# A scaled copy of the rows moved from VectorE to ScalarE, a rest of the context keys moved from GpSimd to VectorE, and first shared weights loaded one stage earlier

## The reference

```python
x = x + tanh(g_xattn[0]) * masked_attention(layernorm(x), ctx, mask, wq, wk, wv, wo, wg)   # 16 heads
x = x + tanh(g_ffn[0])   * ternary_linear(layernorm(x), weight, bias)
# second attention, for each sequence: Q = layernorm(x) [128 x 512], K = V = ctx [128 x 512]
s   = sigmoid(einsum('bdn,bdm->bnm', Q, K) / sqrt(128))        # 512 x 512
x   = x + tanh(g_xattn[1]) * einsum('bvn,bnm->bvm', V, s)
# 16 routed experts (4 for each row) and a shared expert of twice 352 hidden columns
xf  = layernorm(x)
z   = silu(xf @ sw1) * (xf @ sw3) @ sw2
x   = x + tanh(g_ffn[1]) * (routed_experts(xf) + z)
```

## Time and profile before

| | |
|---|---|
| Median of 3 runs | 1314.29 us |
| The profiled execution's own time | 1312.92 us |
| Its span | 1311.2 us |
| PE busy | 1218.4 us, 93% of the span |
| DVE, ACT, POOL busy | 684.4, 556.6, 433.5 us (52%, 42%, 33%) |
| Granted PE clock, mean | 0.979 of full speed |

### The profile page before, as it was taken

How to read it: one execution, slowest core, us unless ns; L and a number is a source line. 1 busy time by engine, 2 the same in 40 slices (tenths; PEclk the granted TensorE clock), 3 DMA queues, 4 the chain that set the end, 5 groups by cost and what they waited for, 6 DMA issues and landing times. The chain is left out here.

```text
span 1311.2 us, 25675 instructions
## 1 busy us (share of the span) xinstructions
PE 1218.4 (93%) x7835; PEld 1024.6 (78%) x7836; DVE 684.4 (52%) x1433; ACT 556.6 (42%) x1355; POOL 433.5 (33%) x518
## 2 busy tenths in 40 slices
PE   6998999999998888958999999899999999999995
PEld 6877787777786566745777787789999889999995
DVE  6556545545545698953656654633234553424241
ACT  4554455455455566723111111543334553434342
POOL 1102211211214466440002762244444344444433
PEclk9999999999999889979999999999999999999998
DMA  9100000000000011043000231665445666645454
GB/s 330 36 17 20 17 1 20 18 1 18 17 17 17 9 30 35 9 140 131 0 1 0 66 131 48 227 163 107 80 80 133 172 148 165 140 86 132 83 141 72
DMA packets 54335, 100.36 MB, mean 77 GB/s; under 512 B 5094, under 2 KB 21990, under 8 KB 54262
## 3 DMA queue, kind: packets, MB, share of 16 engines
q0 software_dynamic: 15824, 37.76, 15.2%
q1 hardware_dynamic: 38438, 61.65, 14.5%
HBM read 72.91 MB, written 26.48 MB: 76 GB/s over the span
## 5 line engine op out<-in xcount | busy, mean ns | idle before, releaser
L1828 PE MATMUL t_H<-m_W,t_xT 128*128 128x352 f32 x1632 | 280.3, 327 | 6.4 <-DVE m_W L1906 4.7
L1828 PEld LDWEIGHTS t_H<-m_W,t_xT 128*128 128x128 f32 x1632 | 261.7, 188 | 9.7 <-DVE m_W L1906 7.3
L1796 POOL DMA_INDIRECT out_dram<-t_ys,t_sid x68 | 109.5, 1610 | 220.9 <-ACT t_ys L1857 113.4
L688 ACT ACTIVATE pr<-SC,neg 128x128 f32<-128x128 f32 x256 | 89.9, 377 | 38.3 <-DVE neg L897 38.3
L1873 ACT ACTIVATE t_sl<-t_H 128x352 f32<-128x352 f32 x68 | 31.5, 463 | 174.0 <-PE t_H L1828 174.0
L46 PE MATMUL t_Y<-m_W,t_hT 128*128 128x512 f32 (+1 forms) x207 | 87.4, 422 | 5.4 <-issue 3.1
L1951 DVE TENSOR_TENSOR t_hT<-t_TH,t_hT 128x384 fp32r<-128x384 f32 x68 | 37.8, 556 | 102.0 <-ACT t_hT L1894 100.8
L1927 DVE TENSOR_TENSOR t_h<-t_H,t_sl 128x352 f32<-128x352 f32 x68 | 35.6, 523 | 103.3 <-ACT t_sl L1873 103.3
L1857 ACT ACTIVATE t_ys<-t_Y,t_wcol 128x512 f32<-128x512 f32 x69 | 47.3, 686 | 93.7 <-PE t_Y L48 93.7
L48 PE MATMUL t_Y<-m_W,t_hT 128*128 128x512 f32 (+1 forms) x207 | 81.7, 395 | 0.0
L47 PE MATMUL t_Y<-m_W,t_hT 128*128 128x512 f32 (+1 forms) x207 | 81.5, 394 | 0.0
(11 more groups left out here) (473 smaller groups left out, 3228.0 us busy)
## 6 DMA issues: line engine op xcount, KB each, us to landing
m_raw<-in_L_ffn_w_dram SPq DMA_DIRECT2D x28, 704.0 KB, 5.3
m_raw<-in_L_ffn_w_dram SPq DMA_DIRECT2D x14, 512.0 KB, 6.7
rows_d<-before_w SPq DMA_DIRECT2D x17, 256.0 KB, 2.0
CT<-in_ctx_dram SPq DMA_DIRECT2D x8, 512.0 KB, 3.6
X<-in_x_dram SPq DMA_DIRECT2D x4, 1024.0 KB, 13.3
out_dram<-X SPq DMA_DIRECT2D x3, 1024.0 KB, 4.3
m_raw<-in_L_ffn_sw_dram SPq DMA_DIRECT2D x4, 704.0 KB, 5.9
m_raw<-in_L_ffn_w_dram SPq DMA_DIRECT2D x14, 192.0 KB, 6.6
```

The lines of the kernel that those rows point to most:

```text
L688: i = act.activation(pr[:, t % 2, slot, :], SC[t % 2][:, slot * S:(slot + 1) * S], ACT.Exp, scale=SCALE0, bias=neg[:, t % 2, slot:slot + 1 ...
L1796: pool.indirect_dma_start(out=m["out_rows"][:, :], out_offset=bass.IndirectOffsetOnAxis(ap=sid[:, b:b + 1], axis=0), in_=ys[:, b, :], in_o ...
L1828: x_ = pe.matmul(bk[b % 2][:, 0:I], xT[:, b % 2, jx, k, :], W13[:, jw, k, j, :], start=k == 0 and jx == jw, stop=k == KC - 1 and jx == 1)
```

## The change

1. `an` (normalised rows in the second attention) and `norm` (in the second block) go from DVE to ACT, as `Identity` with a scale and a bias per row. The bias is minus mean times rstd, made by a new small DVE operation (`shift`, steps `tc`, and one in the second block). `norm` now runs three tiles ahead instead of two, and stands behind ACT's high part of tile t.
2. The low part of the context keys goes from POOL to DVE, as a step of its own: `kl` of tile b+1 stands in round n = 0 of tile b, ahead of the other steps of that round; `kl.0` and `kl.1` stand in the first attention's last group. It raises `ak_lo`, for which the first `aS` of a tile now waits too.
3. `ta` is cut in three: the DVE operations stay (`ta`), POOL's power (`tb`) and DVE's shift (`tc`) come two to six rounds later. In the second block POOL's power stands behind the first two low parts of weights.
4. The first shared weights are loaded in round 28 of the second attention, into space that is free there, and the four `split_hi` stand at tiles 0, 2, 5 and 6; at tile 7 ACT waits for all four low parts. The second shared weights' load no longer waits for them.

```diff
+def shift(dve, c, tiles):
+
+    mean = c["mean"][:, tiles]
+    return dve.scalar_tensor_tensor(out=mean, in0=mean, scalar=-1.0, in1=c["rstd"][:, tiles], op0=ALU.mult, op1=ALU.mult)
+
...
-            "sf.-1 v.2 bc.1 pv.3 on.1 oT.1 pT.8 ta.0 g.2 Sa.5 pT.9 Sb.5 sm.10 sm.11 an.0 qh.0 ks.0 "
-            "oP.1 st.0 pv.4 g.3 pT.10 Sa.6 pT.11 rc.2 Sb.6 sm.12 sm.13 an.1 qh.1 ks.1 "
-            "bc.2 pv.5 on.2 oT.2 st.1 pT.12 v.3 ra.0 Sa.7 pT.13 Sb.7 sm.14 sm.15 "
+            "sf.-1 v.2 bc.1 pv.3 on.1 oT.1 pT.8 ta.0 tb.0 g.2 Sa.5 pT.9 Sb.5 sm.10 sm.11 tc.0 an.0 qh.0 ks.0 "
+            "oP.1 st.0 kl.0 pv.4 g.3 pT.10 Sa.6 pT.11 rc.2 Sb.6 sm.12 sm.13 an.1 qh.1 ks.1 "
+            "bc.2 pv.5 on.2 oT.2 kl.1 st.1 pT.12 v.3 ra.0 Sa.7 pT.13 Sb.7 sm.14 sm.15 "
             "oP.2 aT.0 rb.0 pv.6 aT.1 rd.0 u.0 pT.14 uT.0 aS.0.0 u.1 pT.15 aS.0.1 rc.3 fm.0 ag.0.0 bc.3 pv.7 uT.1 ag.0.1 on.3 oT.3 "
             "aS.0.2 fm.1 oP.3 ", NG - 1)
         between = {0: "sf.-4", 1: "st.-2", 2: "sf.-3", 3: "st.-1", 5: "ra.-1", 6: "rb.-1", 7: "rd.-1 u.-2", 9: "uT.-2", 10: "u.-1",
-                   12: "fm.-2", 13: "uT.-1", 16: "fm.-1", 18: "sf.-2", 20: "sf.-1", 22: "ta.1", 36: "ta.2", 52: "ta.3"}
+                   12: "fm.-2", 13: "uT.-1", 16: "fm.-1", 18: "sf.-2", 20: "sf.-1", 22: "ta.1", 24: "tb.1", 26: "tc.1", 28: "sw", 36: "ta.2", 40: "tb.2",
+                   42: "tc.2", 52: "ta.3", 56: "tb.3", 58: "tc.3"}
         MS = NB * KC
         for m in range(MS):
             b, n = m // KC, m % KC
             text = [between.get(m, "")]
+            if n == 0 and 1 <= b < NB - 1:
+                text += [f"kl.{b + 1}"]
             if m + 3 < MS:
...
-                            sp.wait_ge(aq_lo, b - GB + 1)
+                            sp.wait_ge(ak_lo, b - GB + 1)
                         sp.dma_start(aCX[b % GB], ctx_in[b]).then_inc(ac_in[b % GB], 16)
+                    elif s[0] == "sw":
+                        projected(sp, "g", NB - 1)
+                        projected(sp, "v", NB - 1)
+                        projected(sp, "k", NB // 2 - 1)
+                        r1, r3, r2 = c["shared_raw"]
+                        sp.dma_start(r1, sw1[:, 0:I].rearrange("(k p) i -> p k i", p=P)).then_inc(c["sw13_in"], 16)
+                        sp.dma_start(r3, sw3[:, 0:I].rearrange("(k p) i -> p k i", p=P)).then_inc(c["sw13_in"], 16)
+                        sp.dma_start(r2[:, 0:2, :], sw2[0:2 * P, :].rearrange("(k p) i -> p k i", p=P)).then_inc(c["sw2_in"], 16)
+                        sp.dma_start(r2[0:IC[2], 2, :], sw2[2 * P:I, :]).then_inc(c["sw2_in"], 16)
...
-                    elif kind == "ta":
+                    elif kind == "tb":
...
                         pool.tensor_copy(ak[:, t % 2, 0, :], aCX[t % GB]).then_inc(ak_hi, 1)
-                        pool.wait_ge(ak_hi, t + 1)
-                        pool.tensor_tensor(ak[:, t % 2, 1, :], aCX[t % GB], ak[:, t % 2, 0, :].bitcast(F32), ALU.subtract)
                         pool.wait_ge(aq_hi, t + 1)
                         pool.tensor_tensor(aq[:, t % 2, 1, :], axn[:, t % 2, :], aq[:, t % 2, 0, :].bitcast(F32), ALU.subtract)\
...
                         if n == 0:
                             pe.wait_ge(aq_lo, t + 1)
+                            pe.wait_ge(ak_lo, t + 1)
...
+                    elif kind == "an":
+                        act.wait_ge(a_shift, 1 if t < fresh[0].stop else 2)
+                        if t < 2:
+                            act.wait_ge(t_fill, at(T_KINDS, ("xT", NB - 2 + t)))
+                        else:
+                            act.wait_ge(aq_lo, t - 1)
+                        act.activation(axn[:, t % 2, :], X[:, t, :], ACT.Identity, scale=c["rstd"][:, t:t + 1],
+                                       bias=c["mean"][:, t:t + 1]).then_inc(a_norm, 1)
...
-                    elif kind == "an":
-                        dve.wait_ge(a_powered, 1 if t < fresh[0].stop else 2)
-                        if t < 2:
-                            dve.wait_ge(t_fill, at(T_KINDS, ("xT", NB - 2 + t)))
-                        else:
-                            dve.wait_ge(aq_lo, t - 1)
-                        dve.tensor_scalar(axn[:, t % 2, :], X[:, t, :], c["mean"][:, t:t + 1], c["rstd"][:, t:t + 1],
-                                          ALU.subtract, ALU.mult).then_inc(a_norm, 1)
+                    elif kind == "kl":
+                        dve.wait_ge(ak_hi, t + 1)
+                        dve.tensor_tensor(ak[:, t % 2, 1, :], aCX[t % GB], ak[:, t % 2, 0, :].bitcast(F32), ALU.subtract)\
+                            .then_inc(ak_lo, 1)
+                    elif kind == "tc":
+                        dve.wait_ge(a_powered, t + 1)
+                        shift(dve, c, fresh[t]).then_inc(a_shift, 1)
...
                         else:
                             dve.wait_ge(a_seen, fresh[t].stop)
+                            dve.wait_ge(a_norm, fresh[t].stop)
                         scale_c(t)
...
+        FIRST_SPLIT_AT = (0, 2, 5, 6)
...
-                load(0)
...
-                sp.wait_ge(w_lo, PARTS)
-                load(1)
+                load_second()
...
-                row_power(pool, c, scales, slice(3 * GB, NB), powered)
                 for n in range(PARTS):
+                    if n == 2:
+                        row_power(pool, c, scales, slice(3 * GB, NB), powered)
                     raw, hi, lo = part(0, n)
                     pool.wait_ge(w_hi, n + 1)
                     pool.tensor_tensor(lo, raw, hi.bitcast(F32), ALU.subtract).then_inc(w_lo, 1)
...
+                def norm(t):
+                    if t == 3 * GB:
+                        act.wait_ge(shifted, 1)
+                    if t >= NX:
+                        act.wait_ge(t_fill, t - NX + 1)
+                        act.wait_ge(row_out[t % NX], 16 * (t // NX))
+                    act.activation(xn[:, t % NX, :], X[:, t, :], ACT.Identity, scale=c["rstd"][:, t:t + 1],
+                                   bias=c["mean"][:, t:t + 1]).then_inc(normed, 1)
+                for t in range(3):
+                    norm(t)
...
                     act.wait_ge(t_fill, t + 1)
                     act.activation(XT[:, t // GB, 0, :, t % GB * P:(t % GB + 1) * P], T[t % 2][:, :].rearrange("p (k n) -> p k n", k=KC),
                                    ACT.Copy).then_inc(t_hi, 1)
-                    if t < PARTS:
-                        split_hi(0, t)
+                    if t + 3 < NB:
+                        norm(t + 3)
+                    if t in FIRST_SPLIT_AT:
+                        split_hi(0, FIRST_SPLIT_AT.index(t))
+                    if t == 2 * GB - 1:
+                        act.wait_ge(w_lo, PARTS)
...
-                    if t + 2 < NB:
-                        norm(t + 2)
+                    if t == GB:
+                        dve.wait_ge(powered, 1)
+                        shift(dve, c, slice(3 * GB, NB)).then_inc(shifted, 1)
                     dve.wait_ge(t_hi, t + 1)
                     dve.tensor_tensor(XT[:, t // GB, 1, :, t % GB * P:(t % GB + 1) * P], T[t % 2][:, :].rearrange("p (k n) -> p k n", k=KC),
                                       XT[:, t // GB, 0, :, t % GB * P:(t % GB + 1) * P].bitcast(F32), ALU.subtract).then_inc(t_lo, 1)
```

More of the change, by code:

```diff
@@ L69, in program @@
                      onesB=onesB, nhalf=nhalf, tg=tg)
+        for n in ("sw13_in", "sw2_in"):
+            parts[n] = top.enter_context(nc.semaphore(n))
         for e in ("pool", "sp", "dve", "act"):
             parts[f"passed_{e}"] = top.enter_context(nc.semaphore(f"passed_{e}"))
-        attention_and_ternary(nc, parts, x, g_x, g_f, fw, fb, ctx_in, mask, norm_w, wq, wk, wv, wo, wg)
+        attention_and_ternary(nc, parts, x, g_x, g_f, fw, fb, ctx_in, mask, norm_w, wq, wk, wv, wo, wg, sw1, sw2, sw3)
         experts(nc, parts, gate_w, ebias, w1, w2, w3, sw1, sw2, sw3, out)
@@ L124, in attention_and_ternary @@
         xn = sb("xn", [P, 2, D])
+        with ExitStack() as shortly:
+            sraw = shortly.enter_context(nc.sbuf_tensor("shared_raw", [P, P + RAW], F32))
         xT = sb("xT", [P, 2, 2, KC, 2 * S], F32R)
@@ L295, in attention_and_ternary @@
         ac_in = [sem(f"ac_in{n}") for n in range(GB)]
-        a_norm, aq_hi, ak_hi, aq_lo, as_fill, as_hi, as_lo, as_used, a_scales, a_powered, a_seen = (sem(n) for n in (
-            "a_norm", "aq_hi", "ak_hi", "aq_lo", "as_fill", "as_hi", "as_lo", "as_used", "a_scales", "a_powered", "a_seen"))
+        a_norm, aq_hi, ak_hi, aq_lo, as_fill, as_hi, as_lo, as_used, a_scales, a_powered, a_seen, a_shift, ak_lo = (sem(n) for n in (
+            "a_norm", "aq_hi", "ak_hi", "aq_lo", "as_fill", "as_hi", "as_lo", "as_used", "a_scales", "a_powered", "a_seen", "a_shift", "ak_lo"))
         U_STEPS, F_STEPS, A_STEPS = 6, 8, 7
@@ L1063, in routing_and_shared_expert @@
                                     "meta_ok", "pads_in"))
+        shifted = sem("e_shifted")
         meta_ps = sem("e_meta_ps")
@@ L1333, in split_hi @@
```

(5 more changed lines are left out.)

25 lines of the change are left out of this document (11 added, 14 removed).

## The result

The changed kernel takes 1322.29 us, the median of seven runs (1318.39 to 1323.5); the kernel before takes 1315.33 beside it. The ratio is 1.005, 95% interval [1.0037, 1.0062]: slower by 0.5%, and above the forecast of 1316.3 and its range, 1309.5 to 1320.5. One of the 6 us is not the change's: the forecast started from 1314.29 for the kernel before, and beside the changed kernel that one took 1315.33. The profiled execution took 1320.96 us in a span of 1319.3, so against the 1312.92 of the kernel before it has +8.0 us where the sum said +2.0; this comparison of two profiles is the one that the terms can be held against.

A forecast was written before the change was run, and what follows sets the result against it. It took DVE and waits to bound the second attention's first half, PE the second, paced by a chain. Terms +0.4 - 2.3 + 9.5 - 5.6 = +2.0 us, on 1312.92 plus 1.37, gave 1316.3 us, range 1309.5 to 1320.5.

The forecast's parts named there:

- the chain through `kl`: Late second attention: update of X, statistics, `kl`, then PE's first score product, making a cycle of 7.43 us instead of 6.33.
- Everything behind it is shifted: Second block: the gain at the first logits, less 0.7 given back, carries through to the end as -5.6 us.
- The first rival: Slower: `kl` takes 1.0 or more beside POOL, early tiles give nothing back; typically 1318.3, far end 1320.8; chance 0.25.
- End of the first attention: `an.1` on ACT and `kl.1` on DVE add 1.4 us, other relief gives -1.0: +0.4, between -1 and +1.5.
- Tiles 0 to 6: Second attention, DVE-bound: first cycle -1.0, four middle cycles 32.0 us (+1.6), last -2.9 as POOL's wait goes: -2.3.
- The second rival: Faster: DVE's relief counts, the four early cycles take 26.5 us instead of 32.0; total 1309.8; chance 0.25.
- Tiles 6 to 14: Second attention: six cycles of 7.43 us and two of 8.24 with `ta`, 61.1 instead of 51.58: +9.5.
- the 42 to 43 that were named as a sign: Second attention, second half: PE's busy time for 50 us falls to about 42 to 43 us.
- Second block: Start of the second block: first logits at 571.4 instead of 577.66, 0.7 given back: -5.6, between -7.5 and -4.
- Behind the second block: From the sigmoid behind the gate to the end of the span: no difference, 0.
- `kl` beside POOL's cast: Second attention: `kl` takes 0.96 us beside POOL's rounding of the keys, 0.69 where POOL's copy is over.
- The late range of the chain: Tiles 6 to 14: +7.9 us with `kl` at 0.69 everywhere, +12.1 with it at 1.4.

The follow-up runs named there:

- keys_pool: The changed kernel with the keys' low part back on POOL in its earlier place, row copies still on ACT: 1304.51 us, ratio 0.9918 to the kernel before.
- ta_moved: The changed kernel with the two `ta` of rounds 36 and 52 one round later, so none stands ahead of a `kl`: ratio 1.0025 to the kernel before.
- keys_late_end: keys_earlier with `kl` of tiles 13, 14 and 15 back in the changed kernel's place: ratio 1.0006 to the kernel before.
- keys_earlier: The changed kernel with `kl` two rounds into the tile, for tile b+2, still on DVE: 1307.22 us, ratio 0.9942 to the kernel before.
- keys_early_end: The changed kernel with `kl` of tiles 13, 14 and 15 alone two rounds earlier: ratio 1.0019 to the kernel before.
- load_only: The kernel before with the early load of the first shared weights alone and ACT's wait at tile 7: ratio 0.9959 to the kernel before.
- load_late: keys_pool with the first shared weights loaded at the second block's start, as before: ratio 0.9972 to the kernel before.

## Why the prediction was wrong

The mechanism was right and the outcome wrong: the chain through `kl` was named with its instructions and its cycle of 7.43 us (7.45 to 7.47 measured), but the sum came out at +2.0 instead of +8.0. What failed is that no term of the sum let PE's clock change with the kernel. In the late tiles the fall of the clock behind a wait, 1.5 us, has no term. In the second block the step "Everything behind it is shifted" carried the gain at the first logits (6.3 us forecast, 6.2 measured) on to the end as 5.6, where 3.1 were measured. The first rival, that the new wait outweighs, had the sign and the place right, at 1322.3 and above its far end of 1320.8, but not its two conditions: `kl` took 0.95 beside POOL and not 1.0 or more, and the early tiles did give something back.

- **End of the first attention, +0.4.** Right.
- **Tiles 0 to 6, -2.3.** Measured -1.1. The first cycle took 11.40, as forecast with -1.0. The four middle ones took 33.3 us (462.56 to 495.84), not 32.0, and the whole miss is in the first of them (462.56 to 472.01), 9.45 us where 8.2 were forecast for the longest. Its mean granted clock was 0.64; the kernel before had 0.70 in this cycle, whose 7.12 us PE filled. The last fell from 10.21 to 7.16, as forecast: the 2.96 us wait went. The second rival's case for DVE's relief was true only without the chain: keys_pool has 48.4 us where the kernel before has 53.0.
- **Tiles 6 to 14, +9.5.** Mis-sized: +10.9. Four ordinary cycles were 7.45 to 7.47; two were 7.17, since there no cast of POOL runs beside `kl` and it takes 0.67, which saved 0.5 in all. One `ta` cycle took 8.37 for 8.24. The other took 9.88: the missing term is PE's clock behind its wait of 2.17 us. ta_moved gives both `ta` cycles back, 3.4 us (62.4 to 59.1). PE's busy time in the second half came to 41.28 us, below the 42 to 43 that were named as a sign.
- **Second block, -5.6.** Measured -3.1. The working was right to its last step: first logits 10.5 us behind the start, forecast 10.5. (It counts 2.0 us for four high parts "at 0.6"; the trace has one 0.48 us after the other, so the 2.0 is right.) The step that failed is "Everything behind it is shifted". About 2 of the 5 us were lost again in stretches at a lower clock, which the profiles of the changed kernel and keys_late_end have and those of keys_earlier and keys_early_end don't (57.9 and 57.8, a gain of 5.2). In eight profiles this goes with the place of the last `kl`; the totals don't confirm it, and what does it stays open. The cause named for the gain was right: of the early load and the new order, the load gives it (load_only -4.7, load_late +2.8 against before).
- **Behind the second block, 0.** +1.1 in these two profiles. The same code takes 686.6 to 689.6 us in the thirteen profiles; so this is within what differs from one profile to the next.
- **`kl` beside POOL's cast.** 0.95 against 0.67 to 0.68 alone, forecast 0.96. The Trainium skill (SBUF — State Buffer, "Who interferes with whom") has the two exclude each other for the whole instruction. Here the cast ran from 511.66 to 512.27 and `kl` started at 511.87 and ended at 512.82, 0.55 after the cast, where the rule wants 0.67 or more. The measured size decides: the shorter one.

The misses lie on one side. No term of the sum had PE's clock in it, and the waits that the change put in front of PE could only make it slower; the ends of the range had the durations of `kl` and of DVE, and none for PE's speed behind its own waits. The late range of the chain (+7.9 to +12.1) held; the second block's (-7.5 to -4) did not.

## What to carry to other kernels

An instruction moved to a less busy engine is only free where nobody waits for it: find its consumer, and put it in the stream where the engine has passed the consumer's last other condition with time to spare. Here two rounds earlier were worth 14 us (ratios 1.0050 and 0.9942) with the same instructions. Judge the parts of a change separately, since one tie can hide the gains of the others: the early load alone gave -0.4%, with the later powers and the moved rows it was -0.8%, and with the keys on DVE, in the changed place, +0.5%. And where a change adds waits to TensorE, price the clock behind them too, on the losing side.
